# Turning rows of score maxima with 32x32 block transposes and a DRAM buffer instead of TensorE transposes

## What is computed

```python
q = hidden_states @ Wq                       # per head: 256 x 16
logits = einsum('bhqd,bhkd->bhqk', q_h, k_h) * scale      # text keys, 77 of them
probs = softmax(logits)
text_out = einsum('bhqk,bhkd->bhqd', probs, v_h)
scores = einsum('bhqd,bhkd->bhqk', q_h, ip_k_h) * scale   # the other 179 keys
sem = einsum('bqc,bnc->bqn', softmax(q @ k_text.T * scale) @ text, ip) * scale
ip_probs = softmax(scores + 0.5 * sem) * spatial_mask
out = (text_out + einsum('bhqk,bhkd->bhqd', ip_probs, ip_v_h)) @ Wout + bout + residual
```

## Time and profile before

| | |
|---|---|
| median of 3 runs | 1708.06 us (1701.98 to 1714.18) |
| profiled execution, its own time | 1715.15 us |
| its span, first to last instruction | 1713.0 us |
| mean granted TensorE clock | 0.988 |
| instructions | 42882 |
| TensorE matmuls, busy | 1625.4 us (95%) |
| DVE busy | 1380.9 us (81%) |
| ACT busy | 1033.4 us (60%) |
| GpSimd busy | 833.2 us (49%) |

### The profile page before, as it was taken

The page is one execution under the profiler, slowest core; times in us unless marked ns, Lnnn a source line. Parts: engine busy times, 40 slices in busy tenths (PEclk is TensorE's granted clock), DMA queues, the critical chain, the costliest instruction groups (busy, mean ns, idle before and its releaser), DMA issues.

```text
span 1713.0 us, 42882 instructions
## 1 busy us (share of the span) xinstructions
PE 1625.4 (95%) x14568; PEld 1440.6 (84%) x14568; DVE 1380.9 (81%) x3630; ACT 1033.4 (60%) x2204; POOL 833.2 (49%) x691
## 2 busy tenths in 40 slices
PE   4899999999999999999999999999999999999986
PEld 4788888888888888877888888898889888898965
DVE  4577777777777777866889988999889999999884
ACT  3366665666665666655666666666666666666652
POOL 4422222222222222333577667766677566756663
PEclk9999999999999999998999999999999999999998
DMA  7433343334333433543233323332333223332211
GB/s 204 99 105 109 116 122 112 120 117 122 115 116 114 121 113 117 152 118 90 82 96 100 99 65 87 104 97 81 85 98 103 80 72 97 108 87 55 83 29 41
DMA packets 185985, 172.72 MB, mean 101 GB/s; under 512 B 25760, under 2 KB 185770, under 8 KB 185770
## 3 DMA queue, kind: packets, MB, share of 16 engines
q1 hardware_dynamic: 185770, 169.98, 34.1%
HBM read 110.17 MB, written 57.76 MB: 98 GB/s over the span
## 4 chain that ended last, share of the span: by engine, by line
PE 78%; DVE 9%; ACT 4%; issue 4%; POOL 2%; SPq 2%; DMA 1%; DVEq 0%; ACTq 0%; POOLq 0%
PE MISC L101 25%; PE GP L101 16%; PE NAT L226 9%; PE TR L256 7%; PE PV L303 4%; PE PV L287 4%; PE PV L284 2%; PE PV L306 2%; PE MISC L335 2%; DVE PM L819 2%; DVE TA L806 1%; PE MISC L476 1%; ACT PVS L541 1%; PE PV L244 1%; ACT PH L534 1%
## 5 line engine op out<-in xcount | busy, mean ns | idle before, releaser
L970 POOL TENSOR_TENSOR ZS<-ZP 128x256 f32<-128x256 f32 x267 | 267.2, 1001 | 230.7 <-DVE ZP L813 230.6
L527 ACT ACTIVATE P<-TA 128x512 f32<-128x512 f32 x320 | 202.0, 631 | 269.4 <-DVE TA L806 269.0
L226 PE MATMUL NAT<-KS,QS 65*128 65x256 f32 x1280 | 295.6, 313 | 9.5 <-DMA KS<-qk_parts 5.7
L256 PE MATMUL TR<-QS,KS 69*128 69x256 f32 (+1 forms) x1280 | 272.0, 294 | 0.3 <-DVE TA L806 0.2
L975 POOL TENSOR_TENSOR PARTS<-QKF,PARTS 112x512 fp32r<-112x512 f32 (+3 forms) x96 | 126.7, 1320 | 293.6 <-ACT PARTS L555 293.6
L226 PEld LDWEIGHTS NAT<-KS,QS 65*128 65x128 f32 x1280 | 203.0, 191 | 73.5 <-issue 63.5
L101 PE MATMUL GP<-PH,GH 128*128 128x256 f32 (+1 forms) x960 | 244.2, 285 | 15.9 <-DVE ZP L813 15.9
L813 DVE TENSOR_TENSOR ZP<-GP,PM 128x512 f32<-128x512 f32 x320 | 219.2, 685 | 46.5 <-PE GP L101 43.8
L819 DVE SCALAR_TENSOR_TENSOR PM<-P,PH 128x512 f32<-128x512 f32 x320 | 252.3, 788 | 0.0
L797 DVE TENSOR_REDUCE MX<-NAT 128x2 f32<-128x504 f32 x320 | 216.0, 675 | 33.2 <-PE NAT L226 30.4
L101 PE MATMUL GP<-PH,GL 128*128 128x256 f32 (+1 forms) x960 | 240.9, 279 | 0.0
(11 more groups left out here) (279 smaller groups left out, 3959.9 us busy)
## 6 DMA issues: line engine op xcount, KB each, us to landing
QS<-qk_parts SPq DMA_DIRECT2D x480, 64.0 KB
KS<-qk_parts SPq DMA_DIRECT2D x480, 64.0 KB
qk_parts<-PARTS SPq DMA_DIRECT2D x128, 224.0 KB, 2.8
CT<-in_ctx_t SPq DMA_DIRECT2D x32, 512.0 KB, 4.2
qk_parts<-PARTS SPq DMA_DIRECT2D x64, 192.0 KB, 2.4
QS<-NH SPq DMA_DIRECT2D x480, 4.0 KB
XT<-in_x_t SPq DMA_DIRECT2D x48, 112.0 KB, 2.2
XT<-x_t SPq DMA_DIRECT2D x48, 112.0 KB, 2.3
```

Source lines behind the costliest of these rows:

```text
L226: ins = e.matmul(NAT[s % 2][:, i * T:(i + 1) * T], QS[0:KQ, h, i * 128:(i + 1) * 128], KS[0:KQ, h, :], start=True, stop=True)
L256: ins = e.matmul(TR[s % 2][:, i * S:(i + 1) * S], KS[0:w, h, i * 128:(i + 1) * 128], QS[0:w, h, :], start=True, stop=True)
L527: e.activation(P[:, s % NP, :], TA[:, s % 2, :], ACT.Exp, scale=SCALE).then_inc(q["exp"], 1)
L970: e.tensor_tensor(ZS[s % NZ][:, :], ZP[:, s % 2, 0:S], ZP[:, s % 2, S:2 * S], ALU.add).then_inc(q["zs"], 1)
```

## The change

The maxima of a group no longer pass through TensorE, PSUM and ACT. In slot t = 4g - 7, one slot earlier than before, DVE makes the two parts where the maxima lie (two operations on 128 partitions x 16 elements, 8 in layer 1, each waiting for the one before) and turns them with one transpose of 128 x 32 in blocks of 32x32. SP writes the result to a DRAM buffer in that slot, in pieces of 32 elements, and three slots later (t = 4g - 4, ROWS = 3) waits for that write and loads the rows into QS with one DMA. MX is laid out anew for it. TensorE's, ACT's and the ring's part of the turn, and the wait for `nm` ahead of the PV products of layer 1, go.

```diff
@@ mrows
-    return 64 * (g // 2 + 1) if g < G1 else 32 * G1 + 32 * ((g - G1) // 2 + 1)
+    return 16 * (g // 2 + 1)
@@ tiles
-    MX, NH = sb("MX", [128, 2, 2, 8]), sb("NH", [8, 2, 2, S], F32R)
+    MX, MN, NH = sb("MX", [128, 2, 2, 2 * HG]), sb("MN", [128, 2, 2, 4 * HG], F32R), sb("NH", [128, 2, 8 * HG])
@@ tensor
-            g = due_group(t, HG - LEAD + 1)
-            if g is not None:
-                w = 8 if g < G1 else 4
-                if g < G1 + 2:
-                    k, free = take(("mxt", g), (q["nm"], g + 1), t)
...
-                e.wait_ge(q["mx"], HG * g + HG)
-                for i in range(2):
-                    ins = e.transpose(k[:, i * 128:(i + 1) * 128], MX[:, g % 2, i, 0:w], IDENT[:, :])
-                ins.then_inc(q["mxt"], 1)
...
-                e.wait_ge(q["nm"], min(g + 4, 2 * G1))
@@ scalar
-            g = due_group(t, HG - LEAD + 1)
-            if g is not None:
...
-                e.wait_ge(q["mxt"], g + 1)
-                e.mul(NH[0:w, g % 2, 0, :], ring.bank["rows", g], -1.0).then_inc(q["nh"], 1)
@@ vector
-            g = due_group(t, HG - LEAD + 1)
+            g = due_group(t, HG - LEAD)
             if g is not None:
-                w = 8 if g < G1 else 4
-                e.wait_ge(q["nh"], g + 1)
-                e.scalar_tensor_tensor(NH[0:w, g % 2, 1, :], ring.bank["rows", g], -1.0, NH[0:w, g % 2, 0, :].bitcast(F32),
-                                       ALU.mult, ALU.subtract).then_inc(q["nm"], 1)
+                p, n = g % 2, 2 if g < G1 else 1
+                top = MX[:, p, 0:n, :].rearrange("p n c -> p (n c)")
+                if g >= 2:
+                    e.wait_ge(q["nm"], g - 1)
+                e.wait_ge(q["mx"], HG * g + HG)
+                e.tensor_scalar(MN[:, p, 0, 0:8 * n], top, -1.0, None, ALU.mult).then_inc(q["nh"], 1)
+                e.wait_ge(q["nh"], 2 * g + 1)
+                e.scalar_tensor_tensor(MN[:, p, 1, 0:8 * n], top, -1.0, MN[:, p, 0, 0:8 * n].bitcast(F32), ALU.mult, ALU.subtract).then_inc(q["nh"], 1)
+                if g >= 2:
+                    e.wait_ge(q[f"mxw{p}"], 16 * (g // 2))
+                e.wait_ge(q["nh"], 2 * g + 2)
+                e.transpose(NH[:, p, :], MN[:, p, :, :].rearrange("p n c -> p (n c)").bitcast(F32)).then_inc(q["nm"], 1)
@@ sync
-            g = due_group(t, HG - LEAD + 1)
+            g = due_group(t, HG - LEAD)
+            if g is not None:
+                if g >= 2:
+                    e.wait_ge(q[f"mrow{g % 2}"], mrows(g - 2))
+                e.wait_ge(q["nm"], g + 1)
+                e.dma_start(rows_h[g % 2].rearrange("c (k r) -> k c r", k=4), NH[:, g % 2, :]).then_inc(q[f"mxw{g % 2}"], 16)
+            g = due_group(t, HG - LEAD + ROWS)
             if g is not None:
                 hg, n = g % NGRP, 2 if g < G1 else 1
-                e.wait_ge(q["nm"], g + 1)
-                for part in range(2):
-                    for grp in range(n):
-                        r = KM + n * part + grp
-                        e.dma_start(QS[r:r + 1, HG * hg:HG * hg + HG, :].bitcast(F32),
-                                    NH[HG * grp:HG * grp + HG, g % 2, part, :].bitcast(F32)).then_inc(q[f"mrow{g % 2}"], 16)
+                e.wait_ge(q[f"mxw{g % 2}"], mrows(g))
+                e.dma_start(QS[KM:KM + 2 * n, HG * hg:HG * hg + HG, :].bitcast(F32),
+                            rows_h[g % 2].rearrange("(part grp c) q -> part grp (c q)", part=2, grp=2)[:, 0:n, :]
...
```

More of the change, by code:

```diff
@@ L27 @@
 STACKS = 2 * len(Q_PARTS)
-LEAD = 11
+LEAD, ROWS = 11, 3
 SCALE = float(D) ** -0.5
@@ L114, in whole, with build @@
     return w_dr.rearrange("(k p) n -> p k n", p=128)
-def build(nc, ctx, a, parts_h, sel_h, vall, x1, x1_t, out):
+def build(nc, ctx, a, parts_h, sel_h, rows_h, vall, x1, x1_t, out):
     def tiles(stack):
@@ L179, in build @@
     GP = ring.banks[2]
-    rows = PV[0:4, S:2 * S]
     def take(key, freed, t):
@@ L190, in build @@
     q = semaphores(nc, ctx, "w_q w_k w_v w_o w_rest sel x_in c_in xn_in spilled0 spilled1 spilled2 stack0 stack1 stack2 stack3 stack4 "
-                   "mrow0 mrow1 store store_t fill clear clear_q w_hi w_lo xt_hi xt_lo ct_hi ct_lo qk qk_f qk_hi qk_lo "
-                   "tl tpm texp tp tpt tpts g0 g0s snm sn stm st vm v nat mx mxt nh nm tr sum exp pv pvs ont on "
+                   "mrow0 mrow1 mxw0 mxw1 store store_t fill clear clear_q w_hi w_lo xt_hi xt_lo ct_hi ct_lo qk qk_f qk_hi qk_lo "
+                   "tl tpm texp tp tpt tpts g0 g0s snm sn stm st vm v nat mx nh nm tr sum exp pv pvs ont on "
                    "rec num hs hst ht_hi ht_lo om y yt yts w_cip w_ip once once_s once_q norm rn vall_out "
@@ L783, in _ @@
                 if j == 0 and g >= 2:
-                    e.wait_ge(q["mxt"], g - 1)
+                    e.wait_ge(q["nh"], 2 * (g - 1))
                 if s >= 2:
@@ L788, in _ @@
                 if s < S1:
-                    e.tensor_reduce(MX[:, g % 2, :, j], v[:, :, 0:NT0], AX.X, ALU.max)
+                    e.tensor_reduce(MX[:, g % 2, 0, 2 * j:2 * j + 2], v[:, :, 0:NT0], AX.X, ALU.max)
                     if h == 0:
@@ L793, in _ @@
                         ins = e.tensor_tensor_reduce(TMP[:, k, i, :], v[:, i, NT0:T], SN[:, b % 2, i, :], 1.0, -3.0e38, ALU.add, ALU.max,
[L794 removed]
+                                                     MX[:, g % 2, 1, 2 * j + i:2 * j + i + 1])
                     ins.then_inc(q["mx"], 1)
                 else:
[L797 removed]
+                    e.tensor_reduce(MX[:, g % 2, 0, 2 * j:2 * j + 2], v[:, :, 0:NT], AX.X, ALU.max).then_inc(q["mx"], 1)
             s = t
@@ L1109, in _ @@
         for t in range(T0, T1):
-            g = due_group(t, HG - LEAD + 1)
+            g = due_group(t, HG - LEAD)
[5 more added lines that the diff above has]
+            g = due_group(t, HG - LEAD + ROWS)
             if g is not None:
                 hg, n = g % NGRP, 2 if g < G1 else 1
-                e.wait_ge(q["nm"], g + 1)
-                for part in range(2):
-                    for grp in range(n):
-                        r = KM + n * part + grp
-                        e.dma_start(QS[r:r + 1, HG * hg:HG * hg + HG, :].bitcast(F32),
-                                    NH[HG * grp:HG * grp + HG, g % 2, part, :].bitcast(F32)).then_inc(q[f"mrow{g % 2}"], 16)
+                e.wait_ge(q[f"mxw{g % 2}"], mrows(g))
+                e.dma_start(QS[KM:KM + 2 * n, HG * hg:HG * hg + HG, :].bitcast(F32),
+                            rows_h[g % 2].rearrange("(part grp c) q -> part grp (c q)", part=2, grp=2)[:, 0:n, :]
+                            .rearrange("part grp q -> (part grp) q") if n == 2 else
+                            rows_h[g % 2].rearrange("(part grp c) q -> part grp (c q)", part=2, grp=2)[:, 0, :]).then_inc(q[f"mrow{g % 2}"], 16)
             g = due_group(t, -4 * HG)
@@ L1219, in program @@
     sel = nc.dram_tensor("row_sel", (6, T), F32, kind="Internal").ap()
+    rows = nc.dram_tensor("max_rows", (2, 32, 128), F32, kind="Internal").ap()
     vall = nc.dram_tensor("v_ip", (B * 4, C), F32, kind="Internal").ap()
     with ExitStack() as ctx:
-        build(nc, ctx, a, parts, sel, vall, x1, x1_t, out)
+        build(nc, ctx, a, parts, sel, rows, vall, x1, x1_t, out)
 def kernel(**inputs):
```

3 lines of the change are left out of this document (removed).

## The result

| | before | after |
|---|---|---|
| median | 1711.12 us (1701.98 to 1715.44, 4 runs) | 1808.03 us (1798.75 to 1813.05, 4 runs) |
| ratio | | 1.0552 (95% interval 1.0515 to 1.0588) |
| span of the profiled execution | 1713.0 us | 1811.2 us |
| mean granted TensorE clock | 0.988 | 0.948 |

A forecast was written before the change was run, and what follows sets the result against it. The kernel was taken as bound by TensorE's order of starting matmuls, with short ACT or DVE stretches. Terms -32 - 9 - 4 + 10 = -35 us, less 5 held back, gave 1708 - 30 = 1678 us; range 1655 to 1708.

The forecast's parts named there:

- Part 4: DVE, both layers: three operations take 0.58 us per group where L825 took 0.39; a loss taken as 10 us.
- The bound above: Upper limit on DVE's extra time from the three operations: 0.5 us per group, with 0.19 expected.
- Part 1: TensorE: 160 transpose pairs go, each 0.22 us of the chain of waits; 90% of 35 us, a gain of 32.
- the sum: Total of the forecast's gains and losses: -32 - 9 - 4 + 10 = -35 us, cut to -30.
- second rival: TensorE's transposes were covered by an only slightly shorter path through ACT and DVE; 1703 us, chance 0.09.
- Parts 2 and 3: Layer 0: TensorE's stall behind L825 goes, 9 us gain; ACT's copy L516 goes, 4 us gain.
- such stretches: Places where engines other than TensorE stand close behind the chain and take back some gain; 5 us held back.
- Part 5: SP and DMAs: write lands in about 3 us, SP's cycle is 6.8 us against TensorE's 8.8; no cost.
- third rival: The write to DRAM lands late, so SP's cycle holds up TensorE in layer 0; 1758 us, chance 0.08.
- first rival: DVE becomes the lead in layer 1, its three operations taking 0.32 us each; 1703 us, chance 0.11.

The follow-up runs named there:

- e6: Kernel after with DVE's three operations and SP's write one slot later (t = 4g - 6), same place in the slot; 1769.05 us, 1.0339 of before.
- e7: e1 with TensorE's two transposes per group put back as dead work that nobody reads; 1717.31 us, 1.0027 of before.
- e1: Kernel after without the two split operations; DVE only transposes the maxima, the sign sits in constant rows, second part zero; 1695.12 us, 0.9899 of before.
- e3: Kernel before with two 128x32 block transposes added on DVE per group; 1722.83 us, 1.0042 of before.
- e12: Kernel after with each split operation replaced by a single-input reduction in the same place and slot; 1719.62 us, 1.0027 of before.
- e13: Kernel after with TensorE's two transposes per group put back as dead work; 1797.46 us, 1.0504 of before.
- e2: Kernel before with the two split operations added on DVE per group, on tiles nobody reads; 1748.83 us, 1.0224 of before.

## Why the prediction was wrong

**Part 4 failed, in its durations.** It took 0.19 us for each split operation from L928 and L845, by their size; measured were 0.63 and 0.40 us. Size was the wrong likeness. What counts is the inputs and the neighbour. L928 has two SBUF inputs, but GpSimd is seldom running when it does: its row goes from 109 over 111 to 714 ns, and I had read only the mean of 155. L825 reads one input from PSUM; it takes 401 to 414 ns always, and it was the operation to be replaced. The trace of before had the right rows among the operations from SBUF (min, median, max):

```profile
L868 DVE SCALAR_TENSOR_TENSOR NRM<-ON,NRM x16: 241/740/745, 892.9 to 1694.6; 128x40 f32<-128x40 f32 x16
L928 DVE TENSOR_TENSOR CT<-CT,RN x16: 109/111/714, 725.9 to 1565.7; 128x16 f32<-128x16 f32 x16
L863 DVE TENSOR_SCALAR NRM<-ON x16: 123/424/436, 865.4 to 1686.6; 128x40 f32<-128x40 f32 x16
L819 DVE SCALAR_TENSOR_TENSOR PM<-P,PH x320: 669/681/2428, 784.7 to 1680.2; 128x512 f32<-128x512 f32 x160
```

40 elements cost 740 ns beside GpSimd and 241 without; L863, a tensor_scalar, 427 and 123. PM, the largest DVE term of layer 1's chain, once took 1.7 us more than its median. The bound above should have been 0.7 us for each of the two in layer 1, where GpSimd is busy 136 of 200 us. The sequence would then have been 0.7 + 0.7 + 0.2 = 1.6 us, the addition 1.2 us to a group, more than the 1.0 us that DVE is idle. Measured were 1.32 in layer 1 (0.695 + 0.416 + 0.212) and 1.16 in layer 0. With that bound DVE would have led in layer 1, and nothing would have spoken for a faster kernel there.

**It also left out whom the moved step meets.** Part 4 let layer 0's idle time on DVE, 52 us of 200, cover everything. The time is there, but not in the stretch of the batch where DVE, ACT's SN and TensorE's next product follow one another, and there GpSimd runs too. The timeline of GpSimd for one batch would have shown its work in the slots that the change moves to. e6 prices it: layer 0 is whole again one slot later.

**And it had no price for a late TensorE.** A wait was priced at its own length. In layer 0 TensorE stops 2.2 us for SN. The 57 matmuls of the 10.4 us behind would take 6.2 us at the rate of the next window (146 in 16.0), so some 4.2 us more go there, about twice the stop; this is an estimate that takes the matmuls of both windows as alike. A batch of 20 slots loses 4.0 us net (20 x 0.198), so TensorE makes up a part elsewhere.

**Part 1, right in kind, probably too high.** No TensorE time stands between NAT and TR any more. The pairs are worth 22 us where the sum had 32 (e7 against e1). 22 of 35 us is 63%, not 90%, though the intervals just reach 32. The chain's 0.22 us each is a share of one path, and where another path is only slightly shorter, less comes back. That is a part of the second rival.

**Parts 2 and 3, wrong in effect.** The stall for NH is gone, and ACT's copy too, for 9 + 4 us in the sum. But e7, which has these gains and the pairs of before, is 1 to 8 us slower than before. The stalls moved. In e7, once a batch:

```profile
PE MISC L339 <- DVE GL L750: 13.9, 13, 1.1
PE MISC L382 <- ACT YT L590: 8.0, 13, 0.6
```

The first, at L343, was 4.5 us in 4 waits before. The 45 us of gains in the sum (32 + 9 + 4) gave 17 in e1, whose part on DVE is even shorter than that of before. So not 5 us were to be held back for such stretches but some 28.

**The transpose, right.** 0.211 us in after and 0.202 in e1, where 0.20 was taken.

**Part 5, right.** The waits of SP for the landed write and for DVE:

```profile
SPq L1102 <- DMA max_rows<-NH: 67.3, 77, 2.8
SPq L1096 <- DVE NH L808: 608.9, 152, 9.0
```

Its longest wait for a write is 2.8 us, in half of the groups there is none, and of TensorE's waits only one is for a load, NAT once for KS, 1.9 us; none is for the rows of maxima. The write is issued in 0.53 us and the load in 0.29, where 0.95 was taken for both. The third rival is refuted.

**The first rival** was nearest: ZP and PM do rise in layer 1's chain. But it made the three operations equally slow, at 0.32 us each. e3 and e12 refute that: operations that GpSimd doesn't hold cost next to nothing there, and layer 1 of e12 has the shortest slots of all, 2.750 us. The chance of 0.10 for slower was too low, and the range too narrow on its upper side, by a bound that the profile held.

**What stays open.** The two operations cost 113 us on top of e1 and 38 on top of before, though they last nearly as long in both. The pairs may account for 11 of the 75 us between (e13). In e2 TensorE takes the delay in other and shorter stops. That its results are read by nobody explains little by itself, since in after no wait of TensorE is for the rows either. What makes up the remaining 64 us was not separated.

## To carry to other kernels

Before pricing a small DVE operation, ask how many of its inputs are in SBUF and what GpSimd runs beside it, and read min, median and max of its nearest rows: a median or maximum far above the minimum can be a wait, not work. When a step is moved by a slot, lay the timelines of all engines over the new one. And take a constant that only shifts a softmax row in one part.

## What the runs showed of the hardware

- In after, a DVE operation on 128 x 8 or 128 x 16 fp32 that takes 0.16 us alone ended 0.02 to 0.04 us after the GpSimd operation that was running, in all 166 cases over 0.25 us; the longest took 1.56 us. In before, L868 and L863 with 40 elements ended 0.06 us after it. GpSimd's L978 held none of the 16 that ran inside it. Two reductions with a single input and the block transpose, in the same places, never vary by more than about 0.02 us (e12).
- It holds for a tensor_scalar with one SBUF input too (L802, L863), not only for operations with two. The Trainium skill (VectorE: DVE Perf Modes, § Mode 2×_2P) says that an fp32 tensor_scalar from SBUF to SBUF can read one tensor through both ports; that these two ran in that mode no row shows.
- TensorE stopped for 2.2 us, and its granted clock was 0.53 in the 10 us behind, though it was then busy without a gap. In that stretch a NAT pair took 0.43 us and not 0.24.
- A block transpose of 128 x 32 fp32 takes 0.20 to 0.21 us, beside GpSimd too (139 of the 160 in e12, mean 212 ns with it and 212 without).
